# Second attention of a four-layer transformer kernel: keys loaded by groups of heads, and an exact fallback turned into a loop

## What is computed

```python
q = (x @ Wq.T).reshape(B, S, 32, 16).transpose(0, 2, 1, 3)   # k, v likewise with 8 heads, repeated 4 times
qr, kr = apply_rope(q, cos, sin), apply_rope(k, cos, sin)
draft = einsum('bhqd,bhkd->bhqk', qr, kr) + causal            # causal: -3.4e38 on keys of the future
_, idx = top_k(draft, 128)                                    # the 128 largest keys of each query
scores = draft / 4 + (0 at idx, -3.4e38 elsewhere)
out = einsum('bhqk,bhkd->bhqd', softmax(scores), v)
return out.transpose(0, 2, 1, 3).reshape(B, S, 512) @ Wo.T
```

## Time and profile before

| | |
|---|---|
| median of 3 runs | 2333.65 us (2333.04 to 2333.95) |
| profiled execution | 2337.67 us, of which the span of its instructions 2335.80 us |
| TensorE, matmuls | 1884.8 us busy, 81% of the span |
| VectorE (DVE) | 1568.4 us, 67% |
| ScalarE (ACT) | 1180.0 us, 51% |
| GpSimd (POOL) | 791.7 us, 34% |
| mean granted TensorE clock | 0.883 of full speed |

### The profile page before, as it was taken

The page is one execution under the profiler, slowest core; times in us unless marked ns, Lnnn a source line. Parts: engine busy times, 40 slices in busy tenths (PEclk is TensorE's granted clock), DMA queues, the critical chain, the costliest instruction groups (busy, mean ns, idle before and its releaser), DMA issues. The chain is left out here.

```text
span 2335.8 us, 27456 instructions
## 1 busy us (share of the span) xinstructions
PE 1884.8 (81%) x8426; PEld 1377.3 (59%) x8426; DVE 1568.4 (67%) x3640; ACT 1180.0 (51%) x2963; POOL 791.7 (34%) x511
## 2 busy tenths in 40 slices
PE   5899999899998689997557776855877777677997
PEld 4777777777777568886534443432544434345885
DVE  3677777777777645556337888967888987822335
ACT  3556556556565332323355667645666676152221
POOL 3445545445454246553310111130211111132442
PEclk9999999999999889998756689977878887887998
DMA  4112111121110122221710000023000000001111
GB/s 154 32 44 69 66 51 54 52 79 49 43 65 24 62 81 88 101 81 58 134 29 14 15 14 1 1 28 41 5 16 9 14 15 14 1 1 46 55 41 50
DMA packets 48261, 104.71 MB, mean 45 GB/s; under 512 B 6032, under 2 KB 30992, under 8 KB 43664
## 3 DMA queue, kind: packets, MB, share of 16 engines
q1 hardware_dynamic: 48144, 103.40, 14.9%
HBM read 96.04 MB, written 7.34 MB: 44 GB/s over the span
## 5 line engine op out<-in xcount | busy, mean ns | idle before, releaser
L206 PE MATMUL PS<-XT,AR 128*128 128x512 f32 x2472 | 619.3, 405 | 25.7 <-POOL AR L813 12.3
L206 PE MATMUL PS<-AR 128*128 128x512 f32 (+2 forms) x2568 | 544.0, 366 | 24.8 <-POOL AR L323 13.1
L206 PEld LDWEIGHTS PS<-XT,AR 128*128 128x128 f32 x2472 | 470.6, 193 | 138.6 <-issue 16.5
L206 PEld LDWEIGHTS PS<-AR 128*128 128x128 f32 x2568 | 443.9, 193 | 119.5 <-issue 16.8
L1274 POOL TENSOR_TENSOR AF<-AF 128x512 f32<-128x512 f32 (+3 forms) x64 | 148.4, 2319 | 773.8 <-DVE AF L1474 773.8
L1229 ACT ACTIVATE AF<-PS 128x512 f32<-128x512 f32 x160 | 91.8, 596 | 329.7 <-PE PS L1113 190.0
L1416 DVE MAX8 BF<-PS 128x8 f32<-128x256 f32 (+2 forms) x384 | 195.8, 552 | 33.5 <-PE PS L1103 22.1
L1082 PE MATMUL PS<-AR,XT 48*128 48x128 f32 (+3 forms) x256 | 95.1, 458 | 146.1 <-DVE BF L1340 53.4
L1128 PE MATMUL PS<-AF,BF 128*128 128x512 f32 x320 | 190.9, 707 | 24.3 <-ACT AF L1229 24.3
L567 POOL TENSOR_TENSOR AF<-AF 128x512 f32<-128x512 f32 (+1 forms) x64 | 107.5, 1680 | 168.5 <-DVE AF L698 168.5
L1082 PEld LDWEIGHTS PS<-AR,XT 48*128 48x128 f32 x256 | 52.3, 243 | 185.2 <-issue 76.2
(11 more groups left out here) (173 smaller groups left out, 3516.4 us busy)
## 6 DMA issues: line engine op xcount, KB each, us to landing
AF<-in_mean_w SPq DMA_DIRECT2D x48, 448.0 KB, 3.3
AF<-in_ffn_w SPq DMA_DIRECT2D x14, 1536.0 KB, 6.5
AF<-in_attn_w SPq DMA_DIRECT2D x9, 1536.0 KB, 7.4
XT<-rope_scratch SPq DMA_DIRECT2D x192, 64.0 KB, 2.9
AF<-in_attn_w SPq DMA_DIRECT2D x9, 1024.0 KB, 5.2
AF<-in_ffn_w SPq DMA_DIRECT2D x11, 769.0 KB, 4.2
rope_scratch<-BF SPq DMA_DIRECT2D x20, 256.0 KB, 2.3
AR<-rope_scratch SPq DMA_DIRECT2D x24, 128.0 KB, 4.9
```

The lines of the kernel that those rows point to most:

```text
L206: last = nc.tensor.matmul(dst, lhs(a, c), rhs(m, c), start=(first and k == 0), stop=(k == 3 * n - 1 and not more))
```

## The change

On SP the queries of a tile are issued first. The keys follow in four groups of one key head each (four query heads), each group with a wait of its own: for tiles 8 and 9 on the last list matmul of the four query heads of tile x - 2 that read this key head. So there are 24 key DMAs for a half in place of 6, with the same bytes. There are eight key semaphores in place of two; TensorE waits for one at each quarter of the scores, and GpSimd's negation waits for all four of its half. In `resolve`, the 16 copies of the fallback become a loop over heads, and the list of the eight largest goes to a fixed place.

```diff
-        def keys_read(x):
+        def keys_read(x, h=15):
 
-            return (listed(x, 15, 1) if tile_of(x)[1] > 0 else scored(x, 15)) + 1
+            return (listed(x, h, 1) if tile_of(x)[1] > 0 else scored(x, h)) + 1
...
                     sp.wait_ge(A1["ring_full"], keys_read(x - 3))
-                if n % QT == 0:
-                    if x >= 2:
-                        sp.wait_ge(A1["ring_full"], keys_read(x - 2))
-                    for low in (0, 64):
-                        for a, s in enumerate((0, 1, 0)):
-                            src = scr[b, 4, s].rearrange("(c h) t -> c h t", c=HD1)
-                            sp.dma_start(f32(kst[low + a * HD1:low + (a + 1) * HD1, 4 * hf:4 * hf + 4]),
-                                         src[:, 4 * hf:4 * hf + 4]).then_inc(A1[f"kst{hf}"], 16)
                 for low in (0, 64):
                     for j in range(2):
                         for a, s in enumerate((0, 0, 1)):
...
+                if n % QT == 0:
+                    for g in range(4):
+                        if x >= 2:
+                            sp.wait_ge(A1["ring_full"], keys_read(x - 2, G1 * g + G1 - 1))
+                        for low in (0, 64):
+                            for a, s in enumerate((0, 1, 0)):
+                                src = scr[b, 4, s].rearrange("(c h) t -> c h t", c=HD1)
+                                sp.dma_start(f32(kst[low + a * HD1:low + (a + 1) * HD1, 4 * hf + g]),
+                                             src[:, 4 * hf + g]).then_inc(A1[f"kst{hf}{g}"], 16)
...
             def scores(x, q):
 
                 n, i, hf, W = tile_of(x)
+                pe.wait_ge(A1[f"kst{hf}{q}"], 96 * (n // QT + 1))
                 if q == 0:
-                    pe.wait_ge(A1[f"kst{hf}"], 96 * (n // QT + 1))
                     pe.wait_ge(A1[f"qst{x % 3}"], 16 * 12 * (x // 3 + 1))
...
                 k = kst[64:112, 4 * hf:4 * hf + 4]
-                pool.wait_ge(A1[f"kst{hf}"], 96 * (b + 1))
+                for g in range(4):
+                    pool.wait_ge(A1[f"kst{hf}{g}"], 96 * (b + 1))
...
                     dve.wait_ge(A1["exp"], 4 * x + 2)
-                    for h in range(16):
-                        row, wk = S1[x % 2][:, h, 0:W], work[:, 0:W]
+                    with dve.Fori(0, 16) as h:
+                        row, wk = S1[x % 2][:, bass.ds(h, 1), 0:W].rearrange("p o k -> p (o k)"), work[:, 0:W]
                         v.tensor_copy(wk, row)
                         dve.drain()
                         with dve.Fori(0, TOPK // 8):
-                            v.max(best[:, h, 0:8], wk)
+                            v.max(best[:, 0, 0:8], wk)
                             dve.drain()
-                            v.match_replace(wk, best[:, h, 0:8], wk, TAKEN)
+                            v.match_replace(wk, best[:, 0, 0:8], wk, TAKEN)
                             dve.drain()
```

More of the change, by code:

```diff
@@ L965, in build_kernel @@
         A1 = names("a1", "raw_qkv", "raw_wo", "wq_hi", "wq_lo", "wk_hi", "wk_lo", "wv_hi", "wv_lo", "wo_hi", "wo_lo",
-                   "tables", "vproj", "v", "vz", "stored0", "stored1", "kst0", "kst1", "qst0", "qst1", "qst2", "mask", "mask_r",
+                   "tables", "vproj", "v", "vz", "stored0", "stored1", "kst00", "kst01", "kst02", "kst03",
+                   "kst10", "kst11", "kst12", "kst13", "qst0", "qst1", "qst2", "mask", "mask_r",
                    "ring_full", "ring_free", "kneg", "above", "tiny", "stat", "nmax", "thr", "acc", "cut", "tau",
```

## The result

| | before | after |
|---|---|---|
| median of 4 runs each, us | 2333.80 (2333.04 to 2337.32) | 2307.35 (2305.99 to 2308.59) |
| ratio, 95% interval | | 0.987 (0.9853 to 0.9887) |
| profiled execution, us | 2337.67 | 2305.99 |
| its span, us | 2335.80 | 2304.2 |

The change makes the kernel 26.4 us faster by the medians. 2297 was forecast with a range of 2284 to 2312, so the time lies inside, 10 us above the forecast.

What follows compares the result with a forecast made beforehand. VectorE was taken to set the pace, with stalls at the batch switch and at jumps over the fallback. 9.3 - 22.8 - 23.4 = -36.9 us gave 2300.8 us profiled, 2297 us for the median, range 2284 to 2312.

Steps and rivals of the forecast that it cites:

- Part 1, the switch: At tiles 8 and 9, queries first and keys in separately awaited groups cut VectorE's flag waits to 0.68 us: gain 22.8 us.
- Part 2, the jump: Behind the flag, a loop shortens the skipped fallback, so all twelve gaps become 0.93 us: gain 23.4 us.
- all of it counts: Behind the fallback, ScalarE has more slack than the 2.6 us it would lose, so the whole 23.4 us is saved.
- Rival B: At the fallback, the jump stalls as before because any taken branch waits for code: 2320 us; chance 0.12.
- Part 3, the start: At the stage's start, 36 more key DMAs on SP for x = 0 and 1 delay scores (2, 0): cost 9.3 us.
- I take 0.42: At the start, each small key DMA costs SP 0.42 us of issue, with ends 0.31 and 0.60.
- Rival C: At the start, bytes and not issues set the time, costing 0 to 4 us: 2288 to 2292 us; chance 0.13.
- D: At the start, a small DMA costs as much as a query DMA, 17.9 us late: 2305 us; chance 0.08.
- E: At the start, 48 key DMAs cost 1.57 us each, making it 64.5 us late: 2352 us, slower; chance 0.04.
- F: No effect: switch stalls come from the transfers themselves, and jump and start cancel: 2334 us; chance 0.03.
- I count no gain from the clock: At the switch, no clock term was counted, since TensorE also waits for its flag in ordinary tiles.
- it stands 4.02 over the median: The profiled execution before exceeded the runs' median 2333.65 us by 4.02, turning 2300.8 us profiled into 2297 us.

Runs made afterwards that it cites:

- 127 instructions: Against the changed kernel, the skipped fallback written as a loop of two over eight copies: 2309.88 us, ratio 0.9881 to the kernel before.
- the doubled body: Against the changed kernel, the skipped fallback's sixteen copies written out twice, 451 instructions instead of 22: 2340.74 us, ratio 1.0024 to the kernel before.
- the second pair of profiles: The kernels before and after, each unchanged and profiled once more: medians 2334.92 us before and 2308.37 us after.
- the two kernels with fewer issues: Against the changed kernel, first-batch keys whole ahead of queries: 2294.47 us; or behind queries in two groups of two key heads: 2292.67 us.
- the first two experiments: Kernel before with only the fallback loop: 2314.22 us, ratio 0.9897; changed kernel with sixteen fallback copies put back, so keys alone: 2328.67 us, ratio 0.9967.
- the one with twelve copies: Against the changed kernel, a skipped fallback of twelve copies, 171 instructions, last four heads left out: 2315.56 us, ratio 0.9923 to the kernel before.
- the repeat: The changed kernel run again with nothing altered: 2308.37 us, ratio 0.9878 to the kernel before.

## Why the prediction was right, and where it was off

**Part 1, the switch: right.** 22.8 forecast, 22.8 measured (both waits 0.68 after). Group 3 held nobody up: it is issued by 1527.57 us and its scores begin at 1554.96. GpSimd's negation still comes behind the last normalization of its tile (at 1564.65 us), and line 1438, the cut, is what the flag waits for now.

**Part 2, the jump: right in mechanism, 2.5 us too low.** The term was 23.4 and the gaps lost 25.9. I took 2.8 / 3 = 0.93 us, the mean of before's three short gaps, for all twelve. After, five are 0.85 to 0.94 and seven 0.59 to 0.61, mean 8.7 / 12 = 0.73. Before has none of the lower kind, and with 127 instructions there is none either, so no row could have told. The step "all of it counts", argued from ScalarE's slack alone, is shown by the doubled body: 34.1 us of gaps made 32.4 us of time. By the loop alone it is 21.8 of 25.9, with 5.9 lost behind the last flag. Rival B is out: no short jump stalls.

**Part 3, the start: right in mechanism, mis-sized.** "I take 0.42" was the step. The key DMAs after, issue and then time to landing:

```profile
L1047 SPq DMA_DIRECT2D AR<-rope_scratch x96: 302/420/587, 1144.9 to 1602.8; - x96
...
DMA to landing us min/median/max: 1.7/1.9/2.3
```

The median is 420 ns as before, but that is the length of one issue without the time to the next. The term needed the time from issue to issue, and a set of 24 takes 11.25 us, 0.47 each: 48 x 0.05 = 2.3 us more than the 9.3, against 11.4 measured (13.0 by the second pair of profiles). (The 1.9 us of landing are of the size that the step gave the last wait, 2.9, and don't matter beside it.) Rival C (bytes bound the start) is out by the two kernels with fewer issues, which had the start back at 35.8 and 36.7; rivals D and E by the row of issue times; F by the first two experiments.

**What the sum lacked** was a term: the 5.9 us behind the last flag (9.4 by the second pair), where TensorE's clock is at its lower level through the products of tile 14. "I count no gain from the clock" left a loss open as well. In every profile whose last gap is short (0.92 to 0.94 us) that stretch takes 308 to 309 us; in every one whose last gap is long (3.2 to 3.3 us), the one with twelve copies among them, it takes 299 to 307. So it goes with the last gap. How a gap of 2.4 us more or less would move the clock, and why the clock falls in that place in one kernel and not in the other, stays open; I have not tried it by itself.

So up to the last flag it is -37.1 against -36.9 forecast: +2.1 at the start and -2.5 in the gaps nearly cancel. That the sum is closer than its terms is luck. With the 5.9 us behind it the profiled execution took 2305.99 where the sum said 2300.8, about half of the miss of 10.35. The other half is the step "it stands 4.02 over the median": I took the offset of before's profile over to after, but the profile of after stands 1.4 under its median, which makes 5.4 us. In the later groups before had medians of 2336 to 2338, so that offset was mostly one of the three runs that I had, and the gain against the larger groups is 29 us (29.3 in the repeat).

## What to carry to other kernels

Code that is hardly ever run but jumped over at each step is best kept short: here bodies of 171 instructions and more cost some 3 us more at each jump that went too far, and those of 22 or 127 didn't. When a transfer is split so that its parts can start early, count the issues on the queue where the queue has no slack: at the switch, where SP was idle, 24 small DMAs for each half held nobody up, and at the start the same split cost 11 to 13 us over the two halves, so split only where there is something to wait for. And look at what an issue order puts ahead of the data that is wanted first.

## What the runs showed of the hardware that was not expected

- The cost of a jump is short or long, and the long one does not grow with distance: 3.2 to 4.2 us for bodies of 171, 227 and 451 instructions alike. The short one is 0.58 to 0.95 us over 22 instructions and 0.92 to 1.21 over 127, 171 and 227.
- The instruction queue of VectorE moved one packet for every 128 instructions or so that a short body grew by, though none of them was run: 56 packets with 22, 75 with 227.
- A DMA of 16 rows costs SP as much to issue when it carries a quarter of the bytes: median 420 ns for both. Its landing falls from 4.9 to 1.9 us. From one issue to the next it is 0.47 us in a set of 24.
- What stands behind the last flag is the same code in all kernels and took 299.5 to 309.0 us in their profiles (299.5 and 302.7 for before alone). The time goes with the mean granted clock there: 0.90 at 299.5 us, 0.88 at 302.7 and 0.86 at 308 to 309. An effect of a few us can't be read from the span of one profile; it needs the medians, or a count up to a fixed place.
